# Layer 3's value products write 9 columns instead of 99, and no filler products run on TensorE

## The reference

```python
x = L0_attn_x                      # 8 x 512 x 128
# in each of the four layers:
xn = _layernorm(x, axis=-1)
s = attn_ref(xn, ...)              # L0 recurrent, L1 time mix, L2 state space, L3 below
g = _silu(ffn_ref(xn, ...))        # L0, L3 coupling net; L1 local attention; L2 experts
x = x + s * g
...
# layer 3, attn: 16 heads of 8 channels, 512 queries by 512 keys
scores = jnp.einsum('bhnd,bhmd->bhnm', q, k) / jnp.sqrt(jnp.float32(D))
aw = jax.nn.softmax(scores, axis=-1)
topk = max(1, int(N * TOPK_RATIO))
kth = jax.lax.top_k(aw, topk)[0][..., -1:]
mask = (aw >= kth).astype(aw.dtype)
aws = aw * mask
aws = aws / (aws.sum(-1, keepdims=True) + 1e-08)
o_s = jnp.einsum('bhnm,bhmd->bhnd', aws, v)
...
# the coupling net (gates of layers 0 and 3), three cycles:
tf = _coupling_net(out, ...)       # four products with gelu between
out = out + coupling * _twist(out)
```

## Time and profile before

| | |
|---|---|
| median of 3 runs | 5822.17 us (5820.59 to 5825.25) |
| span of the profiled execution, first to last instruction | 5822.4 us |
| PE busy | 4385.6 us (75%), 16724 instructions |
| PE weight loads busy | 2482.1 us (43%) |
| DVE busy | 4514.1 us (78%) |
| ACT busy | 2924.5 us (50%) |
| POOL busy | 2325.4 us (40%) |
| mean granted clock of TensorE | 0.895 |

### The profile page before, as it was taken

The page is one execution under the profiler, slowest core; times in us unless marked ns, Lnnn a source line. Parts: engine busy times, 40 slices in busy tenths (PEclk is TensorE's granted clock), DMA queues, the critical chain, the costliest instruction groups (busy, mean ns, idle before and its releaser), DMA issues. The chain is left out here.

```text
span 5822.4 us, 60164 instructions
## 1 busy us (share of the span) xinstructions
PE 4385.6 (75%) x16724; PEld 2482.1 (43%) x16724; DVE 4514.1 (78%) x8572; ACT 2924.5 (50%) x5085; POOL 2325.4 (40%) x1980
## 2 busy tenths in 40 slices
PE   5876778767787677876778767787678866788776
PEld 1533435344353443534435344353444524444344
DVE  3678966789657996579965799658995489955898
ACT  3544645446444564445644456444564445645455
POOL 0134631447204562045620456104661046610565
PEclk9998889978899888998889988998889998899888
DMA  2000000000000000000000000000000000000000
GB/s 99 1 1 2 1 3 1 1 2 1 3 1 0 2 1 3 1 1 2 1 3 1 2 1 1 3 1 2 1 1 3 1 2 1 1 3 1 2 1 2
DMA packets 3537, 22.97 MB, mean 4 GB/s; under 512 B 336, under 2 KB 336, under 8 KB 2640
## 3 DMA queue, kind: packets, MB, share of 16 engines
q1 hardware_dynamic: 3152, 18.59, 0.8%
HBM read 16.23 MB, written 2.36 MB: 3 GB/s over the span
## 5 line engine op out<-in xcount | busy, mean ns | idle before, releaser
L1622 POOL TENSOR_SCALAR l_pp<-l_sc,l_m 128x512 f32<-128x512 f32 x496 | 783.4, 1579 | 644.3 <-DVE l_m L1572 596.7
L1572 DVE MAX8 l_m<-l_wk 128x8 f32<-128x512 f32 x1536 | 980.6, 680 | 0.0
L224 PE MATMUL bank<-l_v,l_pt 128*128 128x99 f32 (+1 forms) x5888 | 871.4, 300 | 139.5 <-ACT l_pt L1362 114.7
L224 PEld LDWEIGHTS bank<-l_v,l_pt 128*128 128x128 f32 x5888 | 814.9, 216 | 196.7 <-ACT l_pt L1362 154.0
L1316 PE MATMUL bank<-consts,l_pp 128*128 128x128 f32 x2048 | 390.9, 323 | 526.3 <-POOL l_pp L1629 519.8
L1180 POOL TENSOR_TENSOR l_hc<-l_h,l_cn 128x1024 f32<-128x1024 f32 x128 | 302.3, 2362 | 989.0 <-DVE l_h L1130 989.0
L1316 PEld LDWEIGHTS bank<-consts,l_pp 128*128 128x128 f32 x2048 | 280.2, 165 | 959.7 <-POOL l_pp L1629 828.2
L224 PE MATMUL bank<-l_km,hold 128*128 128x512 f32 x1024 | 652.7, 727 | 43.3 <-DVE l_ol L1539 18.1
L1568 DVE MATCH_REPLACE8 l_wk<-l_m,l_wk 128x512 f32<-128x512 f32 x1024 | 684.1, 675 | 0.0
L1392 ACT ACTIVATE l_sc<-bank 128x512 f32<-128x512 f32 x512 | 303.3, 594 | 739.9 <-PE bank L224 738.5
L1629 POOL TENSOR_TENSOR l_pp<-l_pp,l_ex 128x512 f32<-128x512 f32 x496 | 631.0, 1272 | 26.4 <-ACT l_ex L1399 5.7
(11 more groups left out here) (350 smaller groups left out, 8065.6 us busy)
## 6 DMA issues: line engine op xcount, KB each, us to landing
weights<-weights_dram SPq DMA_DIRECT2D x1, 11014.0 KB, 29.0
hold<-x_dram SPq DMA_DIRECT2D x9, 256.0 KB, 2.6
out_dram<-x SPq DMA_DIRECT2D x9, 256.0 KB, 3.4
consts<-consts_dram SPq DMA_DIRECT2D x1, 1503.0 KB, 32.2
rotary<-consts_dram SPq DMA_DIRECT2D x1, 1024.0 KB, 34.1
```

The costliest lines, as they stand in the source:

```text
L224: return nc.tensor.matmul(o, lhsT, rhs, start=start, stop=stop)
L1572: nc.vector.max(m8[n % RM][:, k + 1], wk_[n % 2][:]).then_inc(S["top"], 1)
L1622: nc.gpsimd.tensor_scalar(pp[n % 2][:], sc[n % RS][:], m8[n % RM][:, 3, 0:1], None, ALU.is_ge).then_inc(S["kept"], 1)
```

## The change

`keep_clock` and its eight calls go. Layer 3's `vt` loses the eleven zeroed places and the memset and wait that go with them, and each value product reads and writes the head's own nine columns. The order of everything that stays is the same on every engine, and so is the number of instructions of a value product.

```diff
-        def keep_clock(b, n):
-
-            for _ in range(n):
-                mm(b[:], C("ident"), rot[:, 0])
...
                         lx.pe(pe)
-                        keep_clock(bank[7], 1)
                         def time_mix(i):
...
                             lf[i].pe(pe)
-                            keep_clock(bank[6], 3)
                             pe.wait_ge(S[f"ffn{i}"], 1)
...
                         lx.pe(pe)
-                        keep_clock(bank[7], 1)
                         pe.wait_ge(S["xn"], 1)
...
                         r.then_inc(S["logits"], 1)
-                        keep_clock(bank[7], 2)
...
                         r.then_inc(S["xproj"], 1)
-                        keep_clock(bank[7], 1)
                         pe.wait_ge(S["xsq"], 1)
                         mm(bank[6][0:96], C("rms"), xr[0:96]).then_inc(S["xms"], 1)
-                        keep_clock(bank[7], 2)
                         pe.wait_ge(S["xd"], 1)
...
-                VW = 11
-                vt = sb("l3_v", [128, NT, H3 + VW, D3 + 1], c)
+                vt = sb("l3_v", [128, NT, H3, D3 + 1], c)
...
                             mm(bank[q][:, 0:384], xn[:, 128 * q:128 * q + 128], W("l3_qkv")).then_inc(S["qkv"], 1)
-                        keep_clock(bank[6], 2)
...
                             for k in range(NT):
-                                r = mm(bank[5][:, 9 * h:9 * (h + VW)], pt[n % 2][:, 128 * k:128 * k + 128],
-                                       vt[:, k, h:h + VW].rearrange("p h d -> p (h d)"),
+                                r = mm(bank[5][:, 9 * h:9 * h + 9], pt[n % 2][:, 128 * k:128 * k + 128], vt[:, k, h],
                                        k == 0, k == NT - 1)
...
-                        pe.wait_ge(S["zeros"], 1)
...
-                        nc.gpsimd.memset(vt[:, :, H3:, :], 0.0).then_inc(S["zeros"], 1)
...
                         lo.pe(pe)
-                        keep_clock(bank[6], 1)
                         pe.wait_ge(S["og2"], 1)
```

More of the change, by code:

```diff
@@ L1473, in outputs @@
                             tt(oo[:, q].rearrange("p (h d) -> p h d", d=D3), o1[:], ol[:, q, :, 0:D3], ALU.add).then_inc(S["oo"], 1)
-                        nc.vector.memset(vt[:, :, 0:H3, D3:D3 + 1], 1.0).then_inc(S["ones"], 1)
+                        nc.vector.memset(vt[:, :, :, D3:D3 + 1], 1.0).then_inc(S["ones"], 1)
                         lx.dve(v)
```

## The result

The changed kernel takes 5963.21 us (median of 4 runs, 5959.65 to 5964.66), the kernel before beside it 5821.38: a ratio of 1.0245, 95% interval 1.023 to 1.0259, 142 us slower. The profiled execution spans 5959.6 us; the time of a run is 2.2 us more than its span.

What follows compares the result with a forecast made beforehand. DVE was taken to set layer 3, the largest part, with PE close behind at half clock. Tile waits 16, less direct gain 5.9, plus clock lost without fillers 84 made 94 us over 5822: 5915, range 5842 to 6045.

Steps and rivals of the forecast that it cites:

- direct gain: Layer 2, product of u: starts sooner without the fillers ahead of it, 5.9 us gained over eight batches.
- Rival A: Lower clock at the norms' ends costs 8 to 10 us per batch, layer 3's stretch little: 5865 to 6000; chance 0.67.
- Narrow products save next to nothing: Layer 3's value products: weight loads hide the columns, so nothing was taken off their duration.
- The clock: Mean granted clock falls to 0.60 to 0.70 in layer 3's stretch and 0.75 to 0.80 over all.
- What that costs in the tiles: Layer 3's tiles: late coupling products make DVE wait 2 us more per batch, 16 in all; bounds 0 and 120.
- layer 3's start: Transposes and first two scores run at the lower clock: 1.0 us per batch, 8 in all.
- rival B: PE becomes layer 3's bound: 6000 to 6100, 6180 at worst; signs: DVE waiting for scores, clock under 0.58; chance 0.15.
- Feed-forward of layer 1: Dense PE products after the norm, twice per batch, lose 1.2 us each to the lower clock: 19 us.
- layer 1's start: Dense projections begin at the lower clock for about 3 us, half of it lost: 1.5 x 8 = 12 us.
- Layer 2's input products: Four products in a row at the lower clock in half the batches, 1.3 us each time: 5 us.
- Layer 2 from router to step size: Chain of three products (u, mean square, step size) loses 2.7 us per batch to the lower clock: 21 us.
- Layer 3's end: Last transposes, values and projection partly at half clock: 1.5 us per batch taken, 12 in all.

Runs made afterwards that it cites:

- dose table: Value products of 9, 54, 126 and 144 columns against the kernel before with 99, all fillers kept: ratios 1.0127, 1.0092, 1.0004 and 0.9998.
- The product of 360 columns: Kernel before with 9-column value products, all fillers kept, plus one extra unread 360-column product ahead of each tile's value products: 5992.14 us, ratio 1.03.
- the run with one filler: Kernel before with one filler instead of two behind layer 2's router: 5824.56 against 5822.23 us, ratio 0.9998.

## Why the prediction was right

The time, 5963, lies in the range of 5842 to 6045, and the cause is the forecast one: PE streams less, its granted clock is lower, and it is late where other engines wait for it. The size was forecast less well, 94 us where 142 came. By layers (the direct gain counted in layer 2) the sum had 7, 31, 20 and 36 us for layers 0 to 3; the traces have 6, 36, 33 and 61. Rival A said "layer 3's stretch little", and that half of it did not hold: the narrow products alone cost 78 us. The range was wide enough for this, and its ends were in part set by hand: neither the 110 of its upper end nor the step from 5858 to 5845 at its lower end has a working. Point by point:

- Narrow products save next to nothing: right, 0.06 to 0.09 us per tile where I had 0 to 0.08, and a weight load with its product takes twice as long at half clock, 0.20 against 0.10 us. By the Trainium skill (TensorE: Matmul & The Clock Gate, LDWEIGHTS), whose load time knows no clock, my estimate for the eight would be 0.86 us at half clock; the trace has 1.56, so it does not agree.
- The 1.72 us of the value products at half clock was read at one place, in front of a coupling product. The usual 1.66 makes a tile 4.39 and PE's reserve 0.17 instead of 0.11; the forecast does not hang on it.
- The clock: 0.60 to 0.70 forecast for layer 3's tiles, 0.73 measured; 0.75 to 0.80 forecast over all, 0.822 measured. The direction was right, the depth overstated.
- What that costs in the tiles is the term of the sum that was mis-sized. I took 16 us; the stretch from first to last MAX8 grew by 54, DVE's waits in it by 50 (60.2 from 9.8). The coupling product is where PE is late first, as I said: 40.6 of the 60.2, at 15 of its 24 products, 2.7 us each. Another 7.8 stand at the second tile's score and belong to layer 3's start, below. The remaining 12 are 13 scores late amid the tiles, and that is the sign for which I had said that the forecast would be wrong and rival B hold. B is indeed part of what happened, though its point (0.58) was not reached: the narrow tile at half clock needs 0.86 + 1.57 + 1.87 = 4.30 us of PE, less than DVE's 4.56, but 6.1 with a coupling product of 1.84 in it. The product of 360 columns shows the same: with more PE time at a better clock the waits at the coupling product more than double.
- Feed-forward of layer 1: 19 forecast, 25 by the dense products (55.7 and 55.8 to 69.2 and 67.4); layer 1's start 12 forecast, 10 measured. Together 31 against 36 for the layer.
- Layer 2's input products: 5 forecast for half the batches at 1.3; measured 14 (28.3 to 42.6), since they begin at half clock in all eight and two of the four products run there at least.
- Layer 2 from router to step size: I forecast +21 for the clock and -6 for the delay gone, +15. Measured -18 to the start of the product of u, +8 from there to the mean square, 0 to the step size's products, +14 over these (15.3 to 29.7), so +4; another +15 stands in the rest of the layer and was not in the sum. What I had called four fillers ahead of u are two, of two instructions each; their time was right. The delay was real and three times what I took, but it paid nothing, as the run with one filler shows.
- Layer 0, 7 forecast, 6 measured. Layer 3's end, 12 forecast, 17 measured; it was put down to the fillers and the columns together, but without fillers it is 1 us shorter and with the narrow products alone 25 longer.
- Layer 3's start: 8 us of loss forecast. The late score came, 7.8 us at the second tile as said, and 8.7 and 9.5 us for the first scores in the two runs with 99 columns and without the layer's own fillers. What I did not have is that the stretch up to the first MAX8 got shorter by 10, so that nothing of the loss is left. This is not a filler's work: the stretch takes either 18.4 to 19.0 us or 16.3 to 16.7, and the mean clock in it goes with that, 0.73 or 0.74 in the longer ones before and 0.81 in the one shorter; with 54 columns and all fillers in place six of eight are short, at 0.82 to 0.90. In the changed kernel it is 0.59 to 0.61 in three long ones and 0.71 in five short ones. Here is the first batch before and in the run without router fillers, whose layer 3 is the same:

```profile
457.80:476.70 18.90, 14.46 (x34) 7.18 (x34) 11.68 (x26) 10.32 (x22) 0.36 (x1) 0.73 0.06 14
...
460.40:476.70 16.30, 12.06 (x33) 6.17 (x34) 11.47 (x25) 10.44 (x22) 0.39 (x1) 0.88 0.06 17
```

Why the level is better in some batches was not tried.

- Direct gain of 6: none to be seen.

The mechanism, less streaming, lower clock, later PE, is shown by the dose table for layer 3 and by the single removals for the fillers. Not shown is why the halves add up to 159 and the whole to 142, and why layer 3's end grows by 25 with the narrow products alone and by 17 in the whole change.

## What to carry to other kernels

Extra columns in a product whose time hardly depends on its width cost almost nothing and can hold TensorE's clock up; the same columns as an instruction of their own cost more than they bring. Measure up to which width this holds: here, fp32 with 128 x 128 weights, from 9 to 126 columns eight instructions grew from 1.57 to 1.70 us at half clock, and at 144 to 1.92. And stop where the engine that leads no longer waits: beyond 99 columns the clock rose and the time did not fall. A filler pays where PE waits a few us and dense work follows in which PE leads; price it by the dense products behind it, not by the wait. An engine that is busy 97% of a stretch and seems to set it can still lose by a slower neighbour: look at the few points where it waits for it, and at how close that neighbour's own sum comes to it.

## What was not expected of the hardware

Eight weight loads, each with its product of 9 columns, take 1.57 us at half clock and 0.81 at the full one: they follow the clock of the array. And the level of the clock at which a layer is entered moves its length in kernels with no edit there: layer 3 up to its first MAX8 takes 16.3 or 18.9 us, which makes 13 us over eight batches without the router fillers. That whole layer is 22 us shorter in this trace (2658.0 to 2636.2), but 10 of them are waits that the one trace of the kernel before has and this one lacks. So a difference of 10 us in one layer of one trace is no finding here.
